# A transformer layer on one core: zero rows released at once, fills on Pool, the first projection inside the last attention group, routing tables in one pass

## The reference

```python
def reference(x, wq, wk, wv, wo, w_router, wg, wu, wd, sg, su, sd):   # x: (2, 1024, 256)
    # attention: 32 query heads of 8, 8 key/value heads
    h = layernorm(x)
    q = (h @ wq).reshape(2, 1024, 32, 8); k, v = h @ wk, h @ wv         # k, v repeated 4 times
    scores = einsum("bhqd,bhkd->bhqk", q, k) / sqrt(8)
    amask = where((j >= i - 128) & (j < i), -1e10, 0)                  # the band BELOW the diagonal is masked out
    x = x + (softmax(scores + amask) @ v).reshape(2, 1024, 256) @ wo
    # 8 experts of 640, the best 2 by sigmoid score, and 2 shared ones
    h = layernorm(x)
    s = sigmoid(h @ w_router.T); w, i = top_k(s, 2); w = w / sum(w)
    out = sum over the two chosen e of w_e * (silu(h @ wg[e].T) * (h @ wu[e].T)) @ wd[e].T
    out += sum over the two shared j of (silu(h @ sg[j].T) * (h @ su[j].T)) @ sd[j].T
    return x + out
```

## Time and profile before

| | |
|---|---|
| median of 3 runs | 953.29 us (952.55 to 953.90) |
| the profiled execution | 952.9 us, of which the span from first to last instruction is 951.2 |
| PE busy | 896.4 us, 94% of the span |
| ACT busy | 583.4 us, 61% |
| DVE busy | 444.9 us, 47% |
| Pool busy | 278.7 us, 29% |
| mean granted TensorE clock | 0.983 of full |
| PE's part of the chain that ended last | 78% |

### The profile page before, as it was taken

One profiled execution on the slowest core, in us unless ns is written; L12 is line 12 of the kernel. 1 busy time (PEld: TensorE's weight loads), 2 busy tenths in 40 slices (PEclk: granted clock), 3 DMA queues, 4 the chain that ended last, 5 costly groups with the idle time before them and its releaser, 6 DMA issues.

```text
span 951.2 us, 24249 instructions
## 1 busy us (share of the span) xinstructions
PE 896.4 (94%) x8221; PEld 570.8 (60%) x8222; DVE 444.9 (47%) x761; ACT 583.4 (61%) x733; POOL 278.7 (29%) x422
## 2 busy tenths in 40 slices
PE   9959999999999999999988999999999999999994
PEld 6513333333333333333346888888887888888883
DVE  7724433444444334444456777656653433434332
ACT  4769999999999999999972423332222222222221
POOL 4403333233233333333330000000012545445442
PEclk9969999999999999999997999999999999999998
DMA  5433445555544455532202207100027864564521
GB/s 178 130 112 103 162 157 206 206 199 196 175 149 159 154 206 206 204 93 90 55 22 66 67 18 238 45 1 23 1 81 256 265 209 98 156 180 127 150 35 22
DMA packets 41951, 123.67 MB, mean 130 GB/s; under 512 B 7608, under 2 KB 22968, under 8 KB 35760
## 3 DMA queue, kind: packets, MB, share of 16 engines
q1 hardware_dynamic: 31152, 110.35, 34.0%
q0 software_dynamic: 7008, 9.70, 5.7%
q10 hardware_dynamic: 3744, 3.02, 1.0%
HBM read 74.03 MB, written 49.02 MB: 129 GB/s over the span
## 4 chain that ended last, share of the span: by engine, by line
PE 78%; ACT 8%; DVE 6%; issue 5%; SPq 1%; DMA 1%; DVEq 0%; POOLq 0%; POOL 0%; ACTq 0%
PE ps L1663 18%; PE ps L1811 14%; PE ps L1616 13%; PE ps L1765 11%; ACT arena L930 7%; PE ps L1830 7%; PE ps L1778 5%; DVE ps L1149 3%; PE ps L1557 2%; PE ps L1821 2%; PE ps L1716 1%; PE ps L1542 1%; PE ps L1792 1%; PE ps L1752 1%; PE ps L1734 1%
## 5 line engine op out<-in xcount | busy, mean ns | idle before, releaser
L930 ACT ACTIVATE arena<-ps 128x1024 f32<-128x1024 f32 x336 | 317.0, 1044 | 6.9 <-PE ps L1616 6.9
L1663 PE MATMUL ps<-arena 128*32 128x256 f32 x4096 | 265.1, 385 | 0.1
L759 POOL TENSOR_SCALAR_AFFINE_SELECT arena<-arena 128x512 f32<-128x512 f32 x240 | 150.0, 638 | 302.3 <-ACT arena L941 203.1
L1616 PE MATMUL ps<-arena 64*128 64x512 bf16 (+1 forms) x1280 | 184.5, 343 | 21.5 <-SPq L545 7.7
L1663 PEld LDWEIGHTS ps<-arena 128*32 128x32 f32 x4096 | 111.8, 109 | 103.1 <-issue 38.2
L1149 DVE COPY_PREDICATED ps<-keep,ps 128x512 f32<-128x512 int32 (+1 forms) x128 | 80.5, 629 | 172.1 <-PE ps L1616 172.1
L1616 PEld LDWEIGHTS ps<-arena 64*128 64x128 bf16 x1280 | 53.7, 94 | 175.4 <-ACT arena L930 82.2
L1811 PE MATMUL ps<-wr_all,x2T 128*128 x648 | 144.9, 364 | 5.7 <-issue 3.6
L1811 PEld LDWEIGHTS ps<-wr_all,x2T 128*128 128x128 f32 x648 | 105.6, 189 | 28.0 <-issue 13.7
L1765 PE MATMUL ps<-x2T,wr_all 128*128 128x512 f32 x480 | 118.8, 399 | 1.2 <-issue 1.2
L941 ACT ACTIVATE arena<-ps 128x1024 f32<-128x1024 f32 x112 | 114.2, 1034 | 8.0 <-DVE ps L1149 3.6
(11 more groups left out here) (187 smaller groups left out, 731.6 us busy)
## 6 DMA issues: line engine op xcount, KB each, us to landing
w_scr<-wr_all SPq DMA_DIRECT2D x24, 1280.0 KB, 7.0
wr_all<-w_scr SPq DMA_DIRECT2D x24, 1280.0 KB, 5.6
raw<-w_experts SPq DMA_DIRECT2D x24, 640.0 KB, 7.1
arena<-q_scr SPq DMA_DIRECT2D x64, 64.0 KB
o_scr<-arena SPq DMA_DIRECT2D x128, 32.0 KB, 1.6
arena<-o_scr SPq DMA_DIRECT2D x16, 256.0 KB, 3.9
raw<-w_shared SPq DMA_DIRECT2D x6, 640.0 KB, 4.2
q_scr<-parts SPq DMA_DIRECT2D x8, 384.0 KB, 2.8
```

The costliest lines, as they stand in the source:

```text
L759: nc.gpsimd.affine_select(out=dst, in_=src, compare_op=ALU.is_ge if own else ALU.is_gt, fill=0.0, base=0, pattern=[[0, REP], [-1 if own el ...
L930: nc.scalar.activation(prob[:, SLOT[unit(a, kt)], :, :].rearrange("p h q -> p (h q)"), score.rearrange("p b x -> p (b x)"), ACT.Exp, scale ...
L1616: return nc.tensor.matmul(ps[:, bank, :].rearrange("p (h q) -> p h q", h=2)[:, :, place * P:(place + tiles) * P], kst[r0:r0 + HALF, s, kt ...
L1663: last = nc.tensor.matmul(ps[32 * h:32 * h + 32, 6 + qc, a % 2 * QW:(a % 2 + 1) * QW], vst[:, s, kt, :], prob[:, SLOT[k], h, :], start=(no ...
```

## The change

Six edits:

1. SP adds the 32 to `st_in` at the very start of its stream instead of behind the second stack's loads.
2. The fills of `qst` and `kst` move from DVE to Pool, behind the fill of `vaug`. Pool's band mask and keep masks, which came when the last rows were normalized, now come after eleven of the twelve third parts are made.
3. PE's idle turns go from 52 + 8 to 30 + 4. For the first chunk DVE copies the second half of the turned rows beside ACT.
4. Chunk 0's sums are loaded after group 10 instead of behind group 14 and inverted one part each in groups 12 to 15. Its projection stands in the last group's products, in front of its last 36 value matmuls, in two halves that go to two other PSUM banks. DVE adds and takes statistics by halves. Its turned rows go to banks 4 and 5. Chunk 1's sums are loaded before the last store of the sums.
5. The tables' operands are float32r: the weight is split in two halves, so that a `tile_hot` has 3 x 40 = 120 columns, and `pos_hot` now lies in `x2T` of the chunks that are done.
6. Pieces of the routing move: counting of tiles to steps 28 and 29, `tiles_first` to 30, `tiles_last` to 32, `slot_rows(1)` to 34, `place_rows(1)` to 35. The tables are made in steps 36 and 37.

The first table moved a step later and both have 120 columns. The core of the diff:

```diff
+XT_BANK = (4, 6, 6, 6)
+FIRST_O = (6, 2 * BUF[NEXP - 3])
-EXP_STEP, RANK_STEP, TABLE_STEPS = 23, 27, (35, 37)
+EXP_STEP, RANK_STEP, TABLE_STEPS = 23, 27, (36, 37)
+HOT = 3
...
             sp.sem_inc(w_split, 2)
+            for s in range(2):
+                sp.sem_inc(st_in[s], 32)
...
             load_stack(1, 1)
-            for s in range(2):
-                sp.sem_inc(st_in[s], 32)
...
-            sp.wait_ge(o_stored[0], 16 * REP * KV + FIRST)
-            load_sums(0)
-            group_io(NG - 1, 1, False, False, False)
-            for c in range(1, NC):
+            for n in range(2 * LOOPED, NG - 1):
+                group_io(n, n % 2, n < SPLIT_PAIRS, n + 1 < NG - 1, n + 2 < NG)
+                if n == 2 * LOOPED:
+                    sp.wait_ge(o_stored[0], 16 * REP * KV + FIRST)
+                    load_sums(0)
+            store_acc(NG - 1, 0)
+            sp.wait_ge(o_stored[1], 16 * REP * KV + FIRST)
+            sp.wait_ge(c_proj, 2 + FIRST)
+            load_sums(1)
+            store_acc(NG - 1, 1)
+            for c in range(2, NC):
...
             pool.wait_ge(vaug_ready, 1)
-            pool.wait_ge(a_xn, 3)
+            nc.gpsimd.memset(qst[:, :, :, :].bitcast(F32), 0.0).then_inc(qst_zero, 1)
+            nc.gpsimd.memset(kst[:, :, :].bitcast(F32), TWO_ONES).then_inc(const, 1)
             pool.wait_ge(qst_zero, 1)
...
-            pool.wait_ge(a_xn, NC)
+            pool.wait_ge(a_p2, NC * 3 - 1)
...
-                for k in range(KD):
+                for k in range(KD if c else 1):
                     nc.scalar.copy(x1T[:, c % 2, k, :], ps[:, k, :]).then_inc(a_xT, 1)
...
-            nc.vector.memset(qst[:, :, :, :].bitcast(F32), 0.0).then_inc(qst_zero, 1)
-            nc.vector.memset(kst[:, :, :].bitcast(F32), TWO_ONES).then_inc(const, 1)
...
+            dve.wait_ge(a_tp, 1)
+            nc.vector.tensor_copy(x1T[:, 0, 1, :], ps[:, 1, :]).then_inc(a_xT, 1)
...
+            for n in range(2 * LOOPED, NG - 1):
+                i = n - 2 * LOOPED - 2
+                group(n, n % 2, n + 2 < NG, (lambda: invert(0, i)) if i >= 0 else (lambda: None))
...
+                link(nc.vector.tensor_tensor(hot[:, :, 2, :], one, over_tiles(w_parts[:, k, 1, :].bitcast(F32), NTILE), ALU.mult))
...
-            idle_turns(7, 52)
+            idle_turns(7, 30)
             transpose_x(0)
-            idle_turns(7, 8)
+            idle_turns(7, 4)
...
+            for t in range(1, LAST_MERGE + 2):
+                turn_of(*last, t, True, False)
+            products_of(*last, LAST_MERGE + 2, False)
+            pe.wait_ge(c_oT, 1)
+            pe.wait_ge(merged, NG * NMERGE)
+            project(0, range(0, 2))
+            products_of(*last, LAST_MERGE + 3, False)
+            pe.wait_ge(s_free, NG * NEXP - 2 + BUFS)
+            project(0, range(2, 4))
+            for t in range(LAST_MERGE + 2, len(TURNS)):
+                if t > LAST_MERGE + 3:
+                    products_of(*last, t, False)
+                values_of(*last, t, True)
...
-                    last = nc.tensor.matmul(ps[:, 6, 0:2 * NTILE], pos_hot[k][:, t, :],
+                    last = nc.tensor.matmul(ps[:, 6, 0:HOT * NTILE], pos_hot[k][:, t // TPC, t % TPC, :],
```

More of the change, by code:

```diff
@@ L1193, in _ @@
                     group(it * 2 + s, s, True)
-            for n in range(2 * LOOPED, NG - 1):
-                group(n, n % 2, n + 2 < NG)
             def x_rows(c, t):
@@ L1278, in _ @@
             merge_pair(NG - 1, 1)
[L1279 to L1280 removed]
+            invert(0, INVERT - 1)
+            normalize(0)
             merge_pair(NG - 1, 2)
@@ L1666, in values, with products_of @@
                 last.then_inc(p_free, 1)
-            def turn_of(n, s, turn, t, before, after):
-                products, ended = TURNS[t]
-                for p in products:
+            def products_of(n, s, turn, t, after):
+                for p in TURNS[t][0]:
                     if not isinstance(p, int):
@@ L1677, in turn_of, with values_of @@
                         scores(n + 1, 1 - s, turn + s, ISSUE_NO[p - NEXP])
-                for v in ended:
+            def values_of(n, s, turn, t, before):
+                for v in TURNS[t][1]:
                     if len(v) == 2:
```

142 lines of the change are left out of this document (82 added, 60 removed).

## The result

| | before | after |
|---|---|---|
| median | 953.69 us (952.55 to 957.94, 6 runs) | 945.33 us (943.38 to 947.60, 6 runs) |
| profiled execution | 952.9, span 951.2 | 946.13, span 944.4 |
| PE busy | 896.4 us | 889.4 us |
| mean granted TensorE clock | 0.983 | 0.987 |

A forecast was written before the change was run, and what follows sets the result against it. PE bounds the kernel; ACT or DVE count only where PE, or at the attention groups ACT, waits. From 952.9 us, 1.1 + 6.2 - 0.3 + 0.75 + 8.1 + 3.3 = 19.15 gives 933.7, range 930.8 to 938.

The forecast's parts named there:

- The fills cost Pool 2.7 us in a stretch in which nobody waits for it: Kernel start: fills moved to Pool delay nobody, since the first stack's load needs them only after two chunks; no cost counted.
- Release, 6.2: Start of attention: with SP's 32 added at once, the first score goes from 57.49 to about 51.25, 6.2 us gained.
- The block in front of the first score, -0.3: Before attention: Pool's masks run beside DVE's last small operations and may hold them; 0.3 us lost.
- my bound of 1.5: Before the first score: two DVE operations held by Pool's masks could lose 0 to 1.5 us.
- Start, 1.1: First projection: fewer idle turns and earlier rows let it begin at about 11.2 instead of 12.30, 1.1 us gained.
- rival B: Start: clock low at the first projection, or DVE blocked at attention's start; costs 1.1 to 1.2 us, 934.9; chance 0.11.
- Last group, 0.75: Last attention group: chunk 0's sums inverted earlier, hidden in DVE's idle time, so ACT's wait shrinks; 0.75 us gained.
- hand-over, 8.1: End of attention: projection before the last value matmuls hides PE's wait and keeps the clock full; 8.1 us gained.
- values lag the masks: Last group: reason given for counting nothing, though the multiply beside Pool's masks may delay these by 0.77 us.
- Tables, 3.3: Routing tables: one-pass products at 0.118 us a pass save 3.76 us, less longer waits and tile counting; 3.3 us gained.
- the moved tile counting: Routing, step 28: the moved counting makes DVE 0.3 us late for chunk 2's last down product.
- the 2.3 forecast: Before the second routing table: DVE falls behind, so PE waits 2.3 us instead of 0.81.

The follow-up runs named there:

- e2: Changed kernel with Pool's two moved fills earlier and the wait for the third chunk's rows back before the one-partition fills; 941.48 us, ratio 0.9866 to the kernel before.
- e1: Kernel before with one edit only: SP adds the 32 at the start of its stream; 947.1 us, ratio 0.9929 to the kernel before.
- e6: e2 with Pool's band and keep masks back behind the last normalized rows; 938.44 us, ratio 0.9836 to the kernel before.
- e7: Changed kernel with DVE's product of chunk 0's sums moved behind the last merge of the last group; 945.49 us, ratio 0.9912 to the kernel before.
- e3: Changed kernel with SP's last store of rows behind the first of the second expert's three loads; 944.67 us, ratio 0.9891 to the kernel before.
- e8: Changed kernel with eight small semaphore instructions on PE before the loop over pairs of tiles; 941.03 us, ratio 0.9871 to the kernel before.
- e12: Changed kernel itself, unaltered, run once more for a second profile; 946.38 us, ratio 0.9910 to the kernel before.
- e5: Changed kernel with tiles_first and tiles_last moved to step 36, behind the second table's operands; 946.11 us, ratio 0.9918 to the kernel before.
- e13: Changed kernel with two small semaphore instructions on PE before the loop over pairs of tiles; one run, 944.57 us.
- e14: Changed kernel with four small semaphore instructions on PE before the loop over pairs of tiles; one run, 943.85 us.
- e4: Changed kernel with PE's idle turns back at 52 and 8; 945.3 us, ratio 0.9891 to the kernel before.
- e9: Changed kernel with the edits of e2, e6, e7 and e8 together; 937.88 us, ratio 0.9825 to the kernel before.
- e11: e9 plus the edits of e3 and e5, with the table read-out also in step 36; 932.89 us, ratio 0.9773 to the kernel before.
- e15: Changed kernel with sixteen small semaphore instructions on PE before the loop over pairs of tiles; one run, 943.28 us.
- e16: Changed kernel with twenty-four small semaphore instructions on PE before the loop over pairs of tiles; one run, 944.66 us.

## Why the prediction was wrong

The direction, and the gains of the release, the hand-over and the tables were right. The sum failed at two steps that were costed at nothing, Pool's fills at the start (4.7) and the routed part (6.3).

- **Start, "The fills cost Pool 2.7 us in a stretch in which nobody waits for it".** This is the step that failed first. Nobody waits for Pool there by a semaphore, but DVE's `tensor_scalar` was blocked until each fill ended. It cost 4.7 us (e2), 3.0 of it idle time and 1.7 the low clock behind. I looked at the moved fills only; most of the block came from the fills of one partition behind them, which the change let run early by taking a wait out, and the prediction does not speak of them. I had the price of such a block in hand for the masks, wrote -0.3 for it there and did not ask the question for the fills.
- **Release, 6.2.** Right: 6.0 alone (e1), 0.2 less.
- **The block in front of the first score, -0.3.** Right in kind, and mis-sized: 0.6 (e6), below my bound of 1.5. I chose 0.3 because the operation has one element; but its size does not matter, what counts is how much of the other's instruction is left. The Trainium skill, "SBUF — State Buffer", section "Who interferes with whom", says this: whoever issues first has the shared ports for its whole instruction, and the other is blocked. The two sums above (20.29 and 20.27, 53.83 twice) agree with it to 0.02 us. The same section names `tensor_scalar` among the operations that can contend with Pool; read for the fills, it would have put the block into the sum.
- **Start, 1.1.** 0.98 in the profile of after. It is less certain than it looks: in the other profiles with 30 turns the projection begins between 10.43 and 12.04, always when the last weights land. The low clock of rival B did not come: the first projection took 5.53 in every profile. What varied was the thirty turns, 4.83 to 6.37 us.
- **Last group, 0.75, and hand-over, 8.1.** Together 8.5 from the merge of pair 1 (473.68, now 472.63) to 513.38, now 503.85, against 8.85. The 0.4 missing is less than what the product beside Pool's selects cost: "values lag the masks" was false, PE waited 0.85 for a select (e7: 0.7).
- **Tables, 3.3.** 3.5. From the up product of step 35 to the first routed product it is 30.0 us instead of 34.1, and 0.6 was lost between the hand-over and there, 0.4 of it in the wait behind the moved tile counting (646.14), for which I had 0.3. The single pass at 120 columns costs 0.123 to 0.125 us, not 0.118, and the first table does not wait at all. The wait of 1.84 before the second is below the 2.3 forecast. But such a wait is a draw: 3 us more when the clock falls (e3).
- **The routed part, not in the sum.** 6.3 given back. 2.9 is the jump back (fifteen times 0.19, e8), which no row of before could show. The other 3.4 is the gather of tile 4, two waits of 1.7 together and the low clock behind them; some 2 of it belong to this profile, since e12 lost only 1.1 there. That index copy followed the first routed matmuls by 19.4 to 21.1 us in the changed kernel's two profiles, in e5, e13 and e14, where PE waited for tile 4, and by 12.7 to 18.7 in before, e1 to e4, e6, e7 and e9 to e11, where it did not. (In e8, e15 and e16 it came after 19.9 to 20.9, but PE had stood idle behind the loop's entry before.) It hangs on SP's loads, which start when the second gather has landed: 3.1 us before the first routed matmuls in the kernel before, 2.1 after. PE had been made faster and the chain of tables, gather and loads had not. I had asked what is late next behind every edit but the last one.

Add up what is missing. Start: 4.7 for the fills, 0.3 more than I took for the block, 0.2 at the release, 0.1 at the projection, together 5.3; last group and hand-over 0.4; tables 0.2 better; routed part 2.9 + 3.4. Another 0.6 was lost inside the first fifteen groups (416.8 us from the first score to the merge of pair 1 in the last, 416.2 before), and its cause is open. That is 12.4, and the span misses 944.4 - 932.1 = 12.3. None of my rivals named the fills or the routed part; B's block in front of the first score came, with 0.3 of the 1.2 that B has for it.

With these mended, the same design takes 932.9 us. Since e11 also takes the wait before the table away, that this is near the forecast is partly chance.

## What to carry to other kernels

An operation that moves to an idle engine is free only if that engine shares nothing with its neighbours: write down what Pool and DVE execute at the same time, and count the longer of the two for the one that comes second. The same question belongs to every wait that is taken out, since what stood behind it now runs beside something else. When PE gets faster in front of a stage that is fed by a chain of other engines (table, index, gather, load), walk that chain too, since its lead is what the gain eats first. And look at the idle time behind loop jumps after any change in the number of instructions ahead of a loop: it is paid at every turn, and it can be moved by a few instructions that do nothing, at 0.15 to 0.17 us each, once.

## What the runs showed of the hardware

- Fills by Pool, which read nothing, block DVE's `tensor_scalar` from SBUF to SBUF in float32: four of 256 columns took 4.57 instead of 1.38 us, most of it beside fills of a single partition. In e2, where these fills ran behind the row operations (21.85), the block is gone. Beside a fill of the same kind, DVE's copy from PSUM (0.69) and its `tensor_tensor` of 512 columns (0.69) were not slowed.
- A DVE product of two SBUF operands and a Pool select held each other nearly to the end: the product, begun 0.41 before a select ended, took 1.49 where it takes 1.22 to 1.26, and the two selects begun 0.92 before the product ended took 2.00 instead of 1.22.
- Float32r matmuls with 120 columns run at 0.123 us each in one pass, 0.119 where PE arrives with no wait (1.90 for sixteen).
- PE's idle time behind a loop's jump was 0.17 or 0.37 us for one and the same loop, by the number of instructions that stand ahead (0.37 with 0, 2 and 4 more, 0.17 to 0.18 with 8, 16 and 24).
- An instruction on PE that only adds 1 to a semaphore took 0.15 to 0.17 us (e8, e14 to e16).
- After one and the same PE wait of 1.83 or 1.84 us the granted clock held in some profiles (the table behind it took 2.00) and fell to half in others (up to 3.59). The runs of one kernel differ in their mean granted clock alike: the changed kernel's six went from 943.4 us at 0.990 to 947.6 at 0.981. My estimate from this is that the medians are uncertain by some 2 us.
